# GIN pass: the edge layer as three products of split operands instead of full f32 operands

## What is computed

```
e   = edge_attr @ W_edge + b_edge            # (50000 x 128) @ (128 x 256)
msg = relu(x[src] + e)
agg = segment_sum(msg, dst)
h   = (1 + eps) * x + agg
h   = relu(h @ W1 + b1) @ W2 + b2            # batch norm, residual and layer norm follow
```

## Time and profile before

| | us |
|---|---|
| median of 3 runs | 3689.67 (3687.28 to 3690.27) |
| profiled execution | 3683.0 |
| its span, first to last instruction | 3681.2 |
| GIN pass in it, about | 60 to 1085 |
| TensorE busy in the span | 3196.1 (87%) |
| ScalarE busy | 2920.5 (79%) |
| VectorE busy | 2819.9 (77%) |
| GpSimd busy | 2373.0 (64%) |

### The profile page before, as it was taken

How to read it: one execution, slowest core, us unless ns; L and a number is a source line. 1 busy time by engine, 2 the same in 40 slices (tenths; PEclk the granted TensorE clock), 3 DMA queues, 4 the chain that set the end, 5 groups by cost and what they waited for, 6 DMA issues and landing times. The chain is left out here.

```text
span 3681.2 us, 88209 instructions
## 1 busy us (share of the span) xinstructions
PE 3196.1 (87%) x24644; PEld 3071.9 (83%) x24644; DVE 2819.9 (77%) x7975; ACT 2920.5 (79%) x6007; POOL 2373.0 (64%) x2467
## 2 busy tenths in 40 slices
PE   4999999999993444459999997999999979999997
PEld 3999999999983444449999997999999979999997
DVE  5999999999986787756666664666666568888886
ACT  1777777777775888858888886788888859999999
POOL 3655555555525666647777775777777677777772
PEclk8999999999996555579999999999999989999999
DMA  4666666666636999967777775777777679999996
GB/s 114 191 178 177 185 181 180 181 181 179 184 113 224 347 353 340 348 196 241 239 236 239 236 239 180 223 241 237 239 238 235 203 247 304 301 299 298 297 297 210
DMA packets 654360, 858.82 MB, mean 233 GB/s; under 512 B 136335, under 2 KB 515882, under 8 KB 654256
## 3 DMA queue, kind: packets, MB, share of 16 engines
q1 hardware_dynamic: 556954, 652.14, 53.7%
q0 software_dynamic: 94080, 205.08, 19.9%
q10 hardware_dynamic: 3222, 0.43, 0.1%
HBM read 639.00 MB, written 257.52 MB: 244 GB/s over the span
## 5 line engine op out<-in xcount | busy, mean ns | idle before, releaser
L492 POOL DMA_INDIRECT rows<-x_in,node_i x490 | 581.3, 1186 | 442.8 <-DVE raw L1046 291.5
L492 POOL DMA_INDIRECT rows<-gb_scratch,node_i x490 | 502.6, 1026 | 198.8 <-issue 133.8
L492 POOL DMA_INDIRECT rows<-x_scratch,node_i x490 | 499.1, 1019 | 188.2 <-issue 130.1
L492 POOL DMA_INDIRECT rows<-ga_scratch,node_i x490 | 499.4, 1019 | 176.7 <-issue 158.4
L504 DVE TENSOR_SCALAR gcn_select<-iota,place 128x256 fp32r<-128x256 f32 (+2 forms) x980 | 365.5, 373 | 221.3 <-ACT gcn_rows_hi L1453 214.7
L520 PE MATMUL gcn_agg_ps<-gcn_select,gcn_rows_hi 128*128 128x256 f32 (+2 forms) x1960 | 502.7, 290 | 18.4 <-DVE gcn_rows_lo L1424 18.4
L534 PE MATMUL gcn_h_ps<-g_hi,gcn_agg_hi 128*128 128x256 f32 x1568 | 456.5, 291 | 62.7 <-ACT gcn_h_ps L1439 61.3
L520 PE MATMUL gcn_agg_ps<-gcn_select,gcn_rows_lo 128*128 128x256 f32 (+2 forms) x1960 | 484.4, 288 | 0.0
L1415 DVE TENSOR_TENSOR gcn_agg_lo<-gcn_agg_ps,gcn_agg_hi 128x1024 fp32r<-128x1024 f32 x196 | 240.0, 1224 | 267.9 <-ACT gcn_agg_hi L1447 267.9
L534 PE MATMUL gcn_h_ps<-g_lo,gcn_agg_hi 128*128 128x256 f32 x1568 | 444.8, 284 | 0.0
L534 PE MATMUL gcn_h_ps<-g_hi,gcn_agg_lo 128*128 128x256 f32 x1568 | 444.1, 283 | 0.0
(11 more groups left out here) (189 smaller groups left out, 11201.9 us busy)
## 6 DMA issues: line engine op xcount, KB each, us to landing
own<-x_t_in SPq DMA_DIRECT2D x196, 256.0 KB, 2.7
h_scratch<-h2t SPq DMA_DIRECT2D x196, 256.0 KB, 3.4
h2t_in<-h_scratch SPq DMA_DIRECT2D x98, 512.0 KB, 5.1
x_sb<-x_q_in SPq DMA_DIRECT2D x98, 512.0 KB, 6.7
x_scratch<-x SPq DMA_DIRECT2D x98, 512.0 KB, 5.6
gcn_own<-x_scratch SPq DMA_DIRECT2D x98, 512.0 KB
ga_scratch<-gcn_h SPq DMA_DIRECT2D x98, 512.0 KB, 3.3
gcn_own<-ga_scratch SPq DMA_DIRECT2D x98, 512.0 KB
```

The lines of the kernel that those rows point to most:

```text
L492: pool.indirect_dma_start(out=c["rows"][0:n, slot, b], out_offset=None, in_=source[:, :], in_offset=bass.IndirectOffsetOnAxis(ap=c["node"] ...
```

## The change

`w_edge` joins the weights that are split. For each pair ScalarE rounds attr to attr_hi (between h0t_hi and the bias copy, lag 2) and VectorE makes attr_lo = attr - attr_hi at the end of its step (lag 2). The edge product is three fp32r matmuls a block instead of one with f32 operands. TensorE no longer waits for the load of attr but for `attr_split`, which VectorE's new instruction gives; ScalarE waits for the load, at lag 2 instead of TensorE at lag 3. attr_hi and attr_lo are double-buffered.

```
-SPLIT = ("w1", "w2", "g1", "g2", "g3")
+SPLIT = ("w_edge", "w1", "w2", "g1", "g2", "g3")
...
+        attr_hi = m.sb("attr_hi", [P, 2, FIRST * P], F32R)
+        attr_lo = m.sb("attr_lo", [P, 2, FIRST * P], F32R)
...
                     if pair := at(3):
                         b = pair.slot % 2
-                        pe.wait_ge(loaded[pair.place], pair.group_landed(2))
+                        pe.wait_ge(attr_split, pair.done())
                         pe.wait_ge(biased, pair.done())
+                        terms = products([attr_hi[:, b], attr_lo[:, b]], [c["w_edge_hi"], c["w_edge_lo"]])
                         for k in range(pair.new):
-                            last = nc.tensor.matmul(edge_ps[:, b, k], attr[:, pair.place, k * P:(k + 1) * P], c["w_edge"][:],
-                                                    start=False, stop=True, skip_group_check=True)
+                            for n, (a, w) in enumerate(terms):
+                                last = nc.tensor.matmul(edge_ps[:, b, k], a[:, k * P:(k + 1) * P], w[:],
+                                                        start=False, stop=n == len(terms) - 1,
+                                                        skip_group_check=True)
                         last.then_inc(edge_done, 1)
...
+                    if pair := at(2):
+                        b = pair.slot % 2
+                        act.wait_ge(loaded[pair.place], pair.group_landed(2))
+                        if pair.has(2):
+                            act.wait_ge(edge_done, pair.before(2))
+                        nc.scalar.copy(attr_hi[:, b, 0:pair.new * P], attr[:, pair.place, 0:pair.new * P]).then_inc(attr_rounded, 1)
...
+                    if pair := at(2):
+                        b = pair.slot % 2
+                        dve.wait_ge(attr_rounded, pair.done())
+                        if pair.has(2):
+                            dve.wait_ge(edge_done, pair.before(2))
+                        nc.vector.tensor_tensor(attr_lo[:, b, 0:pair.new * P], attr[:, pair.place, 0:pair.new * P],
+                                                attr_hi[:, b, 0:pair.new * P].bitcast(F32), ALU.subtract)\
+                            .then_inc(attr_split, 1)
```

More of the change, by code:

```diff
@@ L852, in gin_pass @@
         stored = [m.sem(f"gin_stored{s}") for s in range(RING)]
-        names = ("edge_done select_done rows_added msg_rounded "
+        names = ("attr_rounded attr_split edge_done select_done rows_added msg_rounded "
                  "msg_split biased agg_done h0_done h0_rounded h0_split h1_done h1_ready h1_split h2_done h2_ready stats_done")
-        (edge_done, select_done, rows_added, msg_rounded,
+        (attr_rounded, attr_split, edge_done, select_done, rows_added, msg_rounded,
          msg_split, biased, agg_done, h0_done, h0_rounded, h0_split, h1_done, h1_ready, h1_split, h2_done, h2_ready,
@@ L1693, in gnn @@
             for part in ("_hi", "_lo"):
-                keep[name + part] = m.sb(name + part, [P, 2, D], F32R)
+                keep[name + part] = m.sb(name + part, [P, D] if name == "w_edge" else [P, 2, D], F32R)
         for name in ("b1", "b2", "gamma", "beta"):
```

## The result

The changed kernel takes 3735.04 us (median of 4 runs, 3733.81 to 3740.85), the kernel before 3689.48 in the same count. The ratio is 1.0128 with a 95% interval of 1.0110 to 1.0145: slower by 46 us. The profiled execution took 3734.72 us, its span is 3733.0, 51.8 us longer than before.

A forecast was written before the change was run, and what follows sets the result against it. TensorE was taken to set the GIN pass's pace, VectorE having slack. Locked steps add 1.61 us a group, 39.4 us over 24.5 groups, plus 0.5 for constants: 3723 profiled, 3730 on the median's scale, range 3706 to 3755.

The forecast's parts named there:

- the lock: GIN pass: TensorE's and VectorE's steps each wait for the other's previous step; 43.72 against 42.11 us a group; chance 0.79.
- The table: VectorE's table of edges, made once in eight pairs: its 1.63 us stay and count once in the group's chain.
- DA: VectorE's step behind the table of edges, with 768-column raw: from 4.59 to 5.06 us with the added subtraction.
- DB: VectorE's step with 512-column raw (attr_lo of 256 columns): from 4.81 to 5.14 us with the added subtraction.
- PB: TensorE's step with two edge blocks and three message blocks: 5.10 us with split products, waits apart.
- TensorE to VectorE: Handing over from the end of TensorE's step to VectorE's h: 0.20 us, three times in a group.
- VectorE to TensorE: Handing over from VectorE's attr_lo slot to TensorE's first edge product: 0.19 us, taken between 0.13 and 0.24.
- the lower end of the lock: Whole kernel, 3713 us: handing over at 0.13, subtraction by columns alone, and a select 0.15 us shorter.
- A, no lock: GIN pass: TensorE and VectorE each run on their own sum; 3687 us, no change, or 3670, faster; chance 0.12.
- B, ScalarE late: attr_hi ahead of ScalarE's bias copy delays msg_hi and VectorE stops for it; 22 us more, 3752; chance 0.06.
- C, the clock: TensorE's clock falls in the GIN pass; a tenth of it at 1.2 GHz costs about 90 us, 3820; chance 0.03.
- What costs nothing: ScalarE's attr_hi, at most 0.65 us, covered by 0.87 us idle a step; the earlier attr load lands in time.

The follow-up runs named there:

- the wait without the saving: The change with its wait for attr_split, but TensorE keeps the full f32 edge product and attr_hi and attr_lo are not read: 3747.07 us, ratio 1.0164.
- the work without the wait: The change's added ScalarE and VectorE work, but TensorE keeps the full f32 edge product and waits for the attr load, not attr_split: 3690.55 us, ratio 1.0011.
- with four buffers: The change as it is, with four buffers instead of two for h1t, h1t_hi and h1t_lo: 3725.01 us, ratio 1.0095.
- the change unlocked: The change with only VectorE's attr_lo moved from behind msg_lo to ahead of the batch norm statistics: 3686.47 us, ratio 0.9998.
- the fastest kernel: The change with attr_lo ahead of the statistics, four h1t buffers, and VectorE's table of edges spread in five pieces: 3642.77 us, ratio 0.9897.
- the kernel before with four buffers: The kernel before, full f32 edge product, with four buffers instead of two for h1t, h1t_hi and h1t_lo: 3651.94 us, ratio 0.9919.

## Why the prediction was right, step by step

The forecast was 3730 us with the lock as the cause; 3735 was measured, and the lock is shown: the wait without the saving costs it, the work without the wait does not, and moving attr_lo inside its step removes it.

The terms, as they came out for a group of eight. The table, 1.63 us: 1.63. DA, 5.06: 5.06 (519.20 to 524.26). DB, 5.14: 5.14 (501.57 to 506.71). PB, 5.10: 5.21 with the late second product, which the sum had in the handing over. TensorE to VectorE, 0.20: 0.20 in two of three seams, but 0.37 in the step ahead of the table (512.06 to 512.43). VectorE to TensorE, 0.19: 0.14 (506.71 to 506.85) and 0.11 for the second product, so 0.25, at the upper (0.24) of the two ends that were given. The one wait for ScalarE's h1t that the sum left out: 0.10 (5.32 against 5.21 with four buffers). Together 3 x 0.06 + 0.17 + 0.10 = 0.45 us, and 43.72 + 0.45 = 44.17, what was measured. So the mis-sized term is the handing over, taken between two ends where the trace of before showed the upper one, and taken alike at every seam. With the wait that was left out it put the group at 44.17 us, above the 43.4 to 44.0 that were named as a sign. One bound of the prediction was read too low: by the slope of its rows, (0.87 - 0.60) us for 256 columns, the subtraction by columns alone is 0.41 and 0.27 us, not 0.39 and 0.26, which moves the lower end of the lock by 1 us.

The seam of 0.37 us could have been read ahead: 532.62 in the earlier trace rows is such a step. In the order of instructions with the change it is the one h of a group, other than the one behind the table, where a register instruction takes the wait for agg_done:

```order
L1045 REGISTER_ALU [waits gin_agg_done]
L1048 SCALAR_TENSOR_TENSOR h<-own,self_w,agg_ps 128x512 [waits gin_h0_split,gin_loaded0]
```

That the register instruction makes the 0.17 us is read from this match, not tried.

Of the 2.0 us a group most comes with the table, for which VectorE had slack before. Without it the same chain is four times (0.25 + 5.10 + 0.20 + 5.14) = 42.76 us, and the last whole group, behind the last table, took 42.75 (42.27 before). So 24.5 groups of +2.0 us would be 49 us, and 44.7 came: the last whole group lost 0.5 us, the one ahead of it 1.3, and the first two, where the pipeline fills, 1.2 and 1.6.

That the total was missed by 5 us only is in part luck. A group lost 2.0 us where 1.6 were forecast, 10 us in 24.5 groups, and the start took 3 us more; the groups at both ends gave 4 back. So in the profiles the pass lost 47.8 us, 8 more than the 39.9 of the forecast, while the medians differ by 46.

The start cost 3.1 us and not 0.5. The constants took the 0.5 (22.3 us against 21.8 where the search begins). The rest was overlooked: ScalarE's first activation is now attr_hi, behind the load, and ScalarE's table load (that of its function tables, not of the table of edges) moved with it. The prediction had the first steps wait for gathers; before the change VectorE's first raw waited for the edge product. The kernel before:

```profile
48.69 1.28 ACT L981 ACT_TABLE_LOAD   x1 [48.69 <-issue]
...
63.43 0.96 DVE L1046 TENSOR_TENSOR raw<-edge_ps,rows 128x768 f32<-128x768 f32 x1 [9.82 <-PE edge_ps L917]
```

The change:

```profile
61.69 1.28 ACT L987 ACT_TABLE_LOAD   x1 [61.69 <-DMA attr<-attr_t_in]
...
63.52 0.56 DVE L1099 TENSOR_TENSOR attr_lo<-attr,attr_hi 128x384 fp32r<-128x384 f32 x1 [9.18 <-ACT attr_hi L987]
...
64.34 0.55 PE L921 MATMUL edge_ps<-w_edge_hi,attr_hi 128*128 128x256 f32 x1 [13.98 <-ACT edge_ps L992]
```

Table load, attr_hi, attr_lo and the handing over stand in line between attr's landing and the first product, 61.69 to 64.34. Before, that product started at 60.47.

The rivals. A, no lock: its time (3687) was reached by the runs that open the lock, 3690.55 and 3686.47, which shows that the lock is what the change added; the second has a group of 42.24 us where A's sum for VectorE said 42.0. B, ScalarE late: from 150 to 950 us msg_lo never appears as a waiter in the change. C, the clock: still 1.00 from 150 to 950 us, with TensorE busy 743 of 800. What costs nothing did cost nothing: 0.45 to 0.56 us of attr_hi a step on ScalarE, which still idles 122 us ahead of h1t_hi (133 before). Three split products cost 0.354 us against 0.433 for the f32 block, 0.82 of it.

The Trainium skill's page "FP8 and Floating Point Precision", section "TensorE Precision Notes", with its four passes for true FP32 would make that 0.75; the trace does not agree.

## What to carry to other kernels

In a pipeline of engines that run fixed rows of instructions, an instruction's place in its step decides more than its length: 0.4 us put last on one engine and waited for first on another closed a lock worth 46 us, and the same 0.4 us ahead of the statistics and msg_lo left the time where it was before. Before adding a wait, look whether the awaited engine's step already starts from the waiting engine's last instruction; if so, two steps take the sum of one step of each engine and the two ways over, and work for which one engine had slack, here the table, comes on top. And cheaper work on the engine that sets the pace shows only where it doesn't run into the next wait: of 1.6 us, 0.7 came through, and the rest ran into ScalarE's h1t. Count the end of a pipeline too: the buffers that opened that wait gave 24 us up to the last h and 9 more behind it.

## What the runs showed of the hardware

Handing over cost 0.05 us from VectorE's end to TensorE's first product (506.80 to 506.85), 0.11 us more until TensorE's products followed in their rhythm, and 0.20 us from the start of TensorE's next step to VectorE's start (0.37 us at the one seam of a group where a register instruction takes the wait).

GpSimd's gather instructions were longer in kernels where VectorE had less idle time, though their size is the same. In the kernel before one took 454.19 / 380 = 1.20 us with VectorE busy 735 of 800 us. The list by line (150 to 950 us: busy, mean ns, idle before) has for the change unlocked, with VectorE at 787:

```profile
L492 POOL DMA_INDIRECT rows<-x_in,node_i x379 | 523.0, 1380 | 278.1 <-DVE raw L1057 185.8 <-issue 92.3
```

and for the fastest kernel, with VectorE at 800:

```profile
L492 POOL DMA_INDIRECT rows<-x_in,node_i x388 | 662.3, 1707 | 140.1 <-issue 106.7 <-DVE raw L1082 33.4
```

VectorE's busy time alone does not order them: with VectorE at 751 us in both, a gather took 1.31 us in the run with the wait and without the saving, and 1.19 in the kernel before with four buffers. GpSimd had idle time left in all of them, 140 us in the last, where VectorE waited for its rows once in 800 us, for 0.4 us, so it cost next to nothing here.

The Trainium skill, "SBUF — State Buffer", section "SBUF: two separate sides", describes that GpSimd, while it writes the descriptors of its own transfers, can be locked out of a port that it shares with VectorE by certain VectorE instructions. That could lengthen gathers as seen here, but no run separates it from another cause.
